# State-space stage of a four-layer gated network: the product with B on VectorE, from PSUM, in place of GpSimd

## The chip, the cores and the metric

The kernel runs on one core of a Trainium2 chip. The metric is the device time of one execution in microseconds (us); the kernel before was timed in three runs. TensorE (PE) multiplies matrices, VectorE (DVE), ScalarE (ACT) and GpSimd (POOL) work element by element, SyncE (SP) issues the transfers. Each engine runs its own instructions in their order and waits for semaphores that others raise.

## The reference

Four layers act on a residual x of 1024 tokens by 256; each adds a gated mixer and a gated feed-forward block. The change lies in the first mixer, a selective state-space model. Cut to that:

```python
x = einsum('ed,bld->bel', in_proj_w, ctx)          # 256 channels
u = silu(causal_conv4(x) + conv_b)
x_dbl = einsum('ke,bel->bkl', x_proj_w, u)         # dt (8), B (16), C (16)
delta = softplus(dt_proj_w @ dt + dt_proj_b)
A = -exp(A_log)                                    # 256 x 16
# for every token, in order, per channel e and state n:
dA = exp(delta * A)
state = state * dA + (delta * u) * B
y = sum over n of state * C
# then
out = (y + D * u) * silu(layernorm(residual))
residual = residual + tanh(g) * out
```

All else (a quantised feed-forward block, attention over 16 heads, experts, two more attention and feed-forward layers) comes after this stage and is the same in both kernels.

## The kernel before

The program runs four stages, `ORDER = ["M", "F0", "A1", "F"]`. The change touches stage M, the state-space mixer, alone. Between stages every engine waits in `begin` for `pe_step`, `act_step`, `dve_step` and, for the stages where GpSimd takes part, `pool_step`.

In M the 256 channels lie on 128 partitions times two (`e`), and the 1024 tokens are cut into two halves of 512. The states are taken one at a time: a step `g` of 32 is half `g // 16` and state `g % 16`, and its tiles are 128 x 1024 float32 (two channel groups of 512 tokens). What a step does, by engine:

- TensorE broadcasts row B of the state to all partitions (`broadcast_B`, L406, a matmul with a selector matrix, into PSUM bank 2 or 3 by turns), and row C in the same way (L428, bank 4 or 5). It runs three broadcasts of B ahead. It then adds the step's result to the sum over the states by multiplying with the identity (L434, two matmuls, each recorded as two; banks 0 and 1).
- ScalarE computes `dA`, the exponential, in two instructions (L836), and copies the broadcast B from PSUM to one of three tiles `Bs` in SBUF (`copy_B`, its record is the helper's L750).
- GpSimd multiplies `du` (delta times u) by the copied B into `dBu` (L1656), two tiles by turns.
- VectorE does the recurrence over the tokens as one scan (L1197) on `dA` and `dBu`, and multiplies the state of the step before by the broadcast C straight from PSUM into `hC` (L1204).

The order on VectorE in iteration g is: the scan of g, then the product with C of g - 1, then what is due beside. The order on TensorE in iteration g is: broadcast B for g + 3, broadcast C for g, wait for `m_hC` of g - 1, its identity matmuls, then what is due beside. A broadcast of B waits for the copy of the B two before it, the copy for the product three before it, the product for the scan two before it.

Work of other stages is put beside the loop. Sixteen matmuls of the attention's value weights (L445) stand behind the identity matmuls of the steps in `VALUE_AT`, which are 0, 2, ... 14 and 22 to 29; ScalarE copies each two steps later. Behind step 5 stands a small matmul that sums weight magnitudes (L450), behind step 18 the eight transposes of `output(0)` (L414). On VectorE `gated(0)` (L1181, L1186) stands behind the product of step 16, `residual` (L1087) behind iteration 20, the statistics of the next norm behind 21, `normalise` (L1074) behind 24. GpSimd's `rstd_of()` for that norm is issued behind its product of step 23. Ahead of the loop VectorE finishes `delta(0)` and `delta(1)`, which make `du` for the two halves (L1166, L1167, L1172). After it come `gated(1)`, which waits for the last identity matmuls, and ScalarE's rounding of the first feed-forward weights.

Of the kernel before, what the change touches and what calls it, by code (L numbers as in the profile page):

```python
# [14 lines left out]
def flamingo_kernel(nc, dram, out):  # L15
# [5 lines left out]
    ALU, ACT = mybir.AluOpType, mybir.ActivationFunctionType  # L21
# [181 lines left out]
    def S(name):  # L203
        if name not in sems:
            sems[name] = stack.enter_context(nc.semaphore(name))
        return sems[name]
# [48 lines left out]
    def bc(ap, shape):  # L255
        return ap.to_broadcast(shape)
# [107 lines left out]
    def _(pe):  # L364
# [16 lines left out]
        def ssm(k):  # L381
            loaded(pe, "ctxT", "m_in")
            for h in range(2):
                for e in range(2):
                    last = mm(ps[:, 4 * h + e, :], m_in[:, e * P:(e + 1) * P], ctxT[:, h * HALF:(h + 1) * HALF], start=True, stop=True)
                last.then_inc(S("m_x"), 1)
            loaded(pe, "m_bc", "m_dt", "m_dtw")
            for h in range(2):
                pe.wait_ge(S("m_u"), h + 1)
                for e in range(2):  # L390
                    mm(ps[0:96, 2 + 4 * h, :], m_bc[:, e, :], u[h][:, e, :], start=e == 0, stop=e == 1)
                for e in range(2):
                    last = mm(ps[0:8, 3 + 4 * h, :], m_dt[:, e, :], u[h][:, e, :], start=e == 0, stop=e == 1)
                last.then_inc(S("m_dbl"), 1)
                pe.wait_ge(S("m_dts"), h + 1)
                for e in range(2):
                    last = mm(ps[:, 4 * h + e, :], m_dtw[:, e * P:(e + 1) * P], dts[:, :], start=True, stop=True)
                last.then_inc(S("m_dpre"), 1)
            pe.wait_ge(S("m_bcs"), 2)
            pe.wait_ge(S("m_xs"), 2)  # L400
            loaded(pe, "sel_bc", "ident")

            def broadcast_B(g):
                if g >= 2:
                    pe.wait_ge(S("m_Bcopy"), g - 1)
                mm(ps[:, 2 + g % 2, :], sel_bc[:, g % NS, :], bcs[g // NS][:, :], start=True, stop=True).then_inc(S("m_B"), 1)  # L406

            def output(h):

                pe.wait_ge(S("m_yz"), h + 1)  # L410
                for t in range(TH):
                    b, lb = t // 2, t % 2
                    for e in range(2):
                        last = nc.tensor.transpose(ps[:, 6 + t // 2, (t % 2) * DM + e * P:(t % 2) * DM + (e + 1) * P],  # L414
                                                   u[h][:, e, b * DM + lb * P:b * DM + (lb + 1) * P], ident[:, :])
                return last

            loaded(pe, "wvT0", "wo0")
            broadcast_B(0)
            broadcast_B(1)  # L420
            broadcast_B(2)
            for g in range(2 * NS + 1):
                if g + 3 < 2 * NS:
                    broadcast_B(g + 3)
                if g < 2 * NS:
                    if g >= 2:
                        pe.wait_ge(S("m_hC"), g - 1)
                    mm(ps[:, 4 + g % 2, :], sel_bc[:, NS + g % NS, :], bcs[g // NS][:, :], start=True, stop=True).then_inc(S("m_C"), 1)  # L428
                if g:
                    pe.wait_ge(S("m_hC"), g)  # L430
                    if g == NS + 1:
                        pe.wait_ge(S("m_y_read"), 1)
                    for e in range(2):
                        last = mm(ps[:, e, :], ident[:, :], hC[(g - 1) % 2][:, e, :], start=(g - 1) % NS == 0, stop=(g - 1) % NS == NS - 1)  # L434
                    last.then_inc(S("m_y"), 1)
                if g in VALUE_AT:
                    v = VALUE_AT.index(g)
                    if v == HEADS // 2:
                        loaded(pe, "wvT1", "wo1")
                        pe.wait_ge(S("m_res"), 1)  # L440
                    if v >= 2:
                        pe.wait_ge(S("wvo_copied"), v - 1)
                    if v == 3:
                        pe.wait_ge(S("w_scales"), 1)
                    mm(ps[:, 6 + v % 2, 0:DM], wvT[:, v % (HEADS // 2), :], wo[:, v % (HEADS // 2), :], start=True, stop=True).then_inc(S("wvo_psum"), 1)  # L445
                if g == 5:
                    pe.wait_ge(S("wvo_copied"), 2)
                    pe.wait_ge(S("wabs_part"), 1)
                    pe.wait_ge(S("ones_set"), 1)
                    mm(ps[:, 7, 256:259], ones[:, :], wabs[:, 0:3], start=True, stop=True).then_inc(S("wabs_sum"), 1)  # L450
                if g == NS + 2:
                    pe.wait_ge(S("wvo_copied"), HEADS // 2)
                    output(0).then_inc(S("m_out"), 1)
            pe.wait_ge(S("wvo_copied"), HEADS)
            output(1).then_inc(S("pe_step"), 1)
# [288 lines left out]
    def _(act):  # L744
# [4 lines left out]
        def copy(out_, in_):  # L749
            return A(out_, in_, ACT.Copy)  # L750
# [16 lines left out]
        def ssm(k):  # L767
# [47 lines left out]
                act.wait_ge(S("m_ln"), h + 1)  # L815
                A(inv, lnw, ACT.Exp, scale=-1.0).then_inc(S("m_lnw"), 1)

            def copy_B(g):
                act.wait_ge(S("m_B"), g + 1)
                if g >= 3:  # L820
                    act.wait_ge(S("m_dBu"), g - 2)
                copy(Bs[g % 3][:, :], ps[:, 2 + g % 2, :]).then_inc(S("m_Bcopy"), 1)

            act.wait_ge(S("m_bcs"), 2)
            copy_B(0)
            copy_B(1)
            link(sum_weights(1))
            sum_weights(2).then_inc(S("wabs_part"), 1)
            for g in range(2 * NS):
# [7 lines left out]
                             dlt[h][:, e, :].rearrange("p (b l) -> p b l", b=2)[:, :, 1:DM],  # L837
                             ACT.Exp, scale=negA[:, e, n:n + 1])
                last.then_inc(S("m_dA"), 1)
                if g + 2 < 2 * NS:  # L840
                    copy_B(g + 2)
                if g - 2 in VALUE_AT:
                    v = VALUE_AT.index(g - 2)
                    act.wait_ge(S("wvo_psum"), v + 1)
# [210 lines left out]
    def _(dve):  # L1055
# [53 lines left out]
        def ssm(k):  # L1109
# [67 lines left out]
            def gated(h):  # L1177
# [9 lines left out]
                                           xn[h][:, :, :].rearrange("p (b e) l -> p e b l", e=2)[:, e], ALU.mult)  # L1187
                last.then_inc(S("m_yz"), 1)

            flat = "p e t -> p (e t)"  # L1190
            for g in range(2 * NS + 1):
                if g < 2 * NS:
                    dve.wait_ge(S("m_dA"), g + 1)
                    dve.wait_ge(S("m_dBu"), g + 1)
# [342 lines left out]
    def _(pool):  # L1537
# [67 lines left out]
        for k, s in enumerate(ORDER):  # L1605
# [42 lines left out]
                continue  # L1648
            if s == "M":
                begin(pool, k)  # L1650
                for g in range(2 * NS):
                    pool.wait_ge(S("m_Bcopy"), g + 1)
                    pool.wait_ge(S("m_du"), g // NS + 1)
                    if g >= 2:
                        pool.wait_ge(S("m_h"), g - 1)
                    G.tensor_tensor(dBu[g % 2][:, :, :], du[g // NS][:, :, :], bc(Bs[g % 3][:, :].unsqueeze(1), [P, 2, HALF]),  # L1656
                                    ALU.mult).then_inc(S("m_dBu"), 1)
                    if g == NS + 7:
                        rstd_of()
                pool.wait_ge(S("m_dBu"), 2 * NS)  # L1660
                G.tensor_copy(scratch[:, 16:17], mhalf[:, 0:1]).then_inc(S("pool_step"), 1)

    stack.close()
# [105 lines left out]
```

## Time and profile before

| | us |
|---|---|
| median of 3 runs | 1192.35 |
| lowest, highest | 1190.04, 1193.18 |
| profiled execution, span from its first to its last instruction | 1197.3 |
| busy over the whole span: TensorE | 1019.5 |
| VectorE | 773.8 |
| ScalarE | 649.2 |
| GpSimd | 521.5 |

The profiled execution's own time is known by its span, the last row of the first block; it lies 5 us above the median of the runs. All durations come from that one execution. The loop of stage M begins at 61 us (the first scan) and ends at 212 us (the last product with C). "PEclk" is the clock that TensorE was granted, as a share of 2.4 GHz: 1.00 is the full level, 0.50 the low one of 1.2 GHz, and a number between is the mean of a stretch with both. In the timeline each line is an instruction, or some of the same kind merged (x2, x4), with its start and its length; square brackets hold the engine's idle time before it and who ended it. A float32 matmul has two records, so one step's identity matmuls are four.

### The profile page before, as it was taken

What the parts mean: (1) busy time and instruction counts of PE and PEld (TensorE: products, weight loads), DVE (VectorE), ACT (ScalarE), POOL (GpSimd) and SP (SyncE); (2) the same over time, 40 slices, a digit from 0 to 9 for tenths busy, and PEclk for the clock granted to TensorE, in tenths of its full rate; (3) what the DMA queues carried; (4) which work ended last, traced back from release to release, by engine and by line L of the source; (5) the groups of instructions that cost most, each with busy time, mean ns of one, the idle gap of its engine ahead of it and who ended that gap; (6) DMA issues with size and microseconds to landing.
All of it is one profiled execution on the core that took longest, in us unless ns stands there. A gap on an engine that the chain in (4) does not pass through costs nothing.

```text
span 1197.3 us, 15768 instructions
## 1 busy us (share of the span) xinstructions
PE 1019.5 (85%) x5576; PEld 811.0 (68%) x5576; DVE 773.8 (65%) x1276; ACT 649.2 (54%) x1261; POOL 521.5 (44%) x513
## 2 busy tenths in 40 slices
PE   5367677465899999899987899988999999999898
PEld 1022233134799999799976787867777788778787
DVE  6799999794455555655535655577565666667565
ACT  3834434574577667667653466743656644433443
POOL 0254454002466666556643234334344445334353
PEclk7567878785799999999997999998999999989999
DMA  9000100003400000000004000000000040000000
GB/s 353 22 0 1 53 1 1 0 1 130 185 1 1 1 2 1 1 1 1 1 1 193 1 1 1 1 1 1 1 1 1 11 187 1 1 1 1 1 18 19
DMA packets 4734, 35.84 MB, mean 30 GB/s; under 512 B 1160, under 2 KB 2192, under 8 KB 3152
## 3 DMA queue, kind: packets, MB, share of 16 engines
q1 hardware_dynamic: 4656, 34.83, 7.4%
q8 instruction: 45, 0.74, 0.3%
q14 instruction: 33, 0.27, 0.1%
HBM read 33.78 MB, written 1.05 MB: 29 GB/s over the span
## 4 chain that ended last, share of the span: by engine, by line
PE 52%; DVE 14%; ACT 5%; issue 5%; DVEq 0%; POOL 0%; ACTq 0%; POOLq 0%
PE psum L377 13%; PE psum L379 12%; PE psum L378 12%; PE psum L605 4%; DVE f_h_lo L1515 3%; PE psum L593 2%; PE psum L548 2%; ACT f_silu L1032 2%; DVE f_silu L1498 2%; DVE x_norm L1074 2%; PE psum L552 1%; DVE f_silu L1507 1%; PE psum L669 1%; PE psum L704 1%; ACT a_P L948 1%
## 5 line engine op out<-in xcount | busy, mean ns | idle before, releaser
L377 PE MATMUL psum<-x_norm_T_hi,f_wgu_hi 128*128 128x512 f32 x400 | 178.2, 445 | 0.0
L1507 DVE TENSOR_TENSOR f_silu<-f_silu,psum 128x512 f32<-128x512 f32 x100 | 68.8, 688 | 167.8 <-ACT f_silu L1032 167.8
L379 PE MATMUL psum<-x_norm_T_hi,f_wgu_lo 128*128 128x512 f32 x400 | 161.7, 404 | 0.0
L378 PE MATMUL psum<-x_norm_T_lo,f_wgu_hi 128*128 128x512 f32 x400 | 161.2, 403 | 0.0
L750 ACT ACTIVATE f_h_hi<-f_silu 128x512 fp32r<-128x512 f32 x100 | 63.0, 630 | 172.6 <-DVE f_silu L1498 172.1
L377 PE MATMUL psum<-f_wd_hi,f_h_hi 128*128 128x256 f32 x400 | 121.6, 304 | 13.2 <-DVE f_h_lo L1515 13.1
L1515 DVE TENSOR_TENSOR f_h_lo<-f_silu,f_h_hi 128x512 fp32r<-128x512 f32 x100 | 123.6, 1236 | 3.6 <-ACT f_h_hi L750 3.5
L434 PE MATMUL psum<-m_hC,ident_f 128*128 128x512 f32 x128 | 83.7, 790 | 48.4 <-DVE m_hC L1204 46.1
L1584 POOL TENSOR_TENSOR f_wgu_lo<-f_wa,f_wgu_hi 128x512 fp32r<-128x512 f32 x44 | 56.6, 1287 | 146.4 <-ACT f_wgu_hi L750 146.3
L1656 POOL TENSOR_TENSOR m_dBu<-m_du,m_Bs 128x1024 f32<-128x1024 f32 x32 | 79.0, 2471 | 90.2 <-DVE m_h L1197 34.9
L378 PE MATMUL psum<-f_wd_lo,f_h_hi 128*128 128x256 f32 x400 | 114.1, 285 | 0.0
L379 PE MATMUL psum<-f_wd_hi,f_h_lo 128*128 128x256 f32 x400 | 113.8, 285 | 0.0
L1584 POOL TENSOR_TENSOR f_wgu_lo<-f_w,f_wgu_hi 128x512 fp32r<-128x512 f32 x44 | 56.6, 1287 | 103.8 <-ACT f_wgu_hi L750 103.7
L377 PEld LDWEIGHTS psum<-f_wd_hi,f_h_hi 128*128 128x128 f32 x400 | 77.3, 193 | 23.6 <-issue 21.0
L1032 ACT ACTIVATE f_silu<-psum 128x512 f32<-128x512 f32 x100 | 59.1, 591 | 62.7 <-PE psum L379 56.7
L1629 POOL TENSOR_TENSOR a_P<-a_P,a_row_inv 128x1024 f32<-128x1024 f32 x32 | 60.7, 1896 | 71.6 <-DVE a_row_inv L1357 71.6
L379 PEld LDWEIGHTS psum<-x_norm_T_hi,f_wgu_lo 128*128 128x128 f32 x400 | 77.7, 194 | 18.4
L378 PEld LDWEIGHTS psum<-x_norm_T_lo,f_wgu_hi 128*128 128x128 f32 x400 | 78.5, 196 | 15.8
L377 PEld LDWEIGHTS psum<-x_norm_T_hi,f_wgu_hi 128*128 128x128 f32 x400 | 79.2, 198 | 14.6 <-POOL f_wgu_lo L1584 0.2
L434 PEld LDWEIGHTS psum<-m_hC,ident_f 128*128 128x128 f32 x128 | 26.7, 229 | 88.3 <-DVE m_hC L1204 63.8
L378 PEld LDWEIGHTS psum<-f_wd_lo,f_h_hi 128*128 128x128 f32 x400 | 77.5, 194 | 3.9 <-issue 1.4
L379 PEld LDWEIGHTS psum<-f_wd_hi,f_h_lo 128*128 128x128 f32 x400 | 77.4, 193 | 0.0
(297 smaller groups left out, 2794.1 us busy)
## 6 DMA issues: line engine op xcount, KB each, us to landing
f_wa<-in_f1a SPq DMA_DIRECT2D x1, 8448.0 KB, 24.8
f_w<-in_f3w SPq DMA_DIRECT2D x1, 5376.0 KB, 17.0
w_raw<-in_w0raw SPq DMA_DIRECT2D x1, 3072.0 KB, 16.2
f_w<-in_f2w SPq DMA_DIRECT2D x1, 3072.0 KB, 14.5
f_wb<-in_f1b SPq DMA_DIRECT2D x1, 2304.0 KB, 8.2
a_wo<-in_wo SPq DMA_DIRECT2D x2, 1024.0 KB, 12.0
a_wq<-in_wq SPq DMA_DIRECT2D x1, 2048.0 KB, 24.6
x_res<-in_x SPq DMA_DIRECT2D x1, 1024.0 KB, 7.8
```

Of the source, the lines that this page charges most:

```text
L377: mm(out, wh, xh, start=start, stop=False, **kw)
L378: mm(out, wh, xl, start=False, stop=False, **kw)
L379: return mm(out, wl, xh, start=False, stop=stop, **kw)
L434: last = mm(ps[:, e, :], ident[:, :], hC[(g - 1) % 2][:, e, :], start=(g - 1) % NS == 0, stop=(g - 1) % NS == NS - 1)
L605: last = mm(ps[:, 4, b * DM:(b + 1) * DM], ctk[:, ((i - 1) // HEADS) * TH + 2 * b + kv, :], PT[:, b, kv * DM:(kv + 1) * DM], start=kv == 0 ...
L750: return A(out_, in_, ACT.Copy)
L1032: A(sg[g % 2][:, :], ps[:, 2 + 2 * (g % 2), :], ACT.Silu).then_inc(S("f_sg"), 1)
L1507: V.tensor_tensor(sg[g % 2][:, :], sg[g % 2][:, :], ps[:, 3 + 2 * (g % 2), :], ALU.mult).then_inc(S("f_m"), 1)
L1515: V.tensor_tensor(hl[(g - 1) % 2][:, :], sg[(g - 1) % 2][:, :], hh[(g - 1) % 2][:, :].bitcast(f32), ALU.subtract).then_inc(S("f_hl"), 1)
L1584: G.tensor_tensor(wgl[g % 2][:, :], raw_w(l, j)[:, 0:GU], wgh[g % 2][:, :].bitcast(f32), ALU.subtract).then_inc(S("f_wg"), 1)
L1629: G.tensor_tensor(Pm[i % 2][:, :, :], Pm[i % 2][:, :, :], bc(ri[:, :].unsqueeze(2), [P, TH, DM]), ALU.mult).then_inc(S("a_pn"), 1)
L1656: G.tensor_tensor(dBu[g % 2][:, :, :], du[g // NS][:, :, :], bc(Bs[g % 3][:, :].unsqueeze(1), [P, 2, HALF]), ALU.mult).then_inc(S("m_dBu"), 1)
```

## The change

VectorE gets a new function, `input_term(g)`, that multiplies `du` by the broadcast B read from PSUM and writes `dBu`. It is issued one step ahead: for step 0 before the loop, and for g + 1 at the head of iteration g, ahead of the scan of g. GpSimd's product and ScalarE's copy of B are gone, and with them the wait of the broadcast for the copy: it now waits for the product two steps before it. TensorE's broadcast of B runs one step ahead of its iteration in place of three: two before the loop, then B for g + 1 at the head of iteration g. GpSimd's `rstd_of()` comes first in its stage.

```diff
--- before.py
+++ after.py
@@ -402,7 +402,7 @@
 
             def broadcast_B(g):
                 if g >= 2:
-                    pe.wait_ge(S("m_Bcopy"), g - 1)
+                    pe.wait_ge(S("m_dBu"), g - 1)
                 mm(ps[:, 2 + g % 2, :], sel_bc[:, g % NS, :], bcs[g // NS][:, :], start=True, stop=True).then_inc(S("m_B"), 1)
 
             def output(h):
@@ -418,10 +418,9 @@
             loaded(pe, "wvT0", "wo0")
             broadcast_B(0)
             broadcast_B(1)
-            broadcast_B(2)
             for g in range(2 * NS + 1):
-                if g + 3 < 2 * NS:
-                    broadcast_B(g + 3)
+                if g and g + 1 < 2 * NS:
+                    broadcast_B(g + 1)
                 if g < 2 * NS:
                     if g >= 2:
                         pe.wait_ge(S("m_hC"), g - 1)
@@ -815,15 +814,6 @@
                 act.wait_ge(S("m_ln"), h + 1)
                 A(inv, lnw, ACT.Exp, scale=-1.0).then_inc(S("m_lnw"), 1)
 
-            def copy_B(g):
-                act.wait_ge(S("m_B"), g + 1)
-                if g >= 3:
-                    act.wait_ge(S("m_dBu"), g - 2)
-                copy(Bs[g % 3][:, :], ps[:, 2 + g % 2, :]).then_inc(S("m_Bcopy"), 1)
-
-            act.wait_ge(S("m_bcs"), 2)
-            copy_B(0)
-            copy_B(1)
             link(sum_weights(1))
             sum_weights(2).then_inc(S("wabs_part"), 1)
             for g in range(2 * NS):
@@ -837,8 +827,6 @@
                              dlt[h][:, e, :].rearrange("p (b l) -> p b l", b=2)[:, :, 1:DM],
                              ACT.Exp, scale=negA[:, e, n:n + 1])
                 last.then_inc(S("m_dA"), 1)
-                if g + 2 < 2 * NS:
-                    copy_B(g + 2)
                 if g - 2 in VALUE_AT:
                     v = VALUE_AT.index(g - 2)
                     act.wait_ge(S("wvo_psum"), v + 1)
@@ -1187,8 +1175,19 @@
                                            xn[h][:, :, :].rearrange("p (b e) l -> p e b l", e=2)[:, e], ALU.mult)
                 last.then_inc(S("m_yz"), 1)
 
+            def input_term(g):
+                dve.wait_ge(S("m_du"), g // NS + 1)
+                dve.wait_ge(S("m_B"), g + 1)
+                if g >= 2:
+                    dve.wait_ge(S("m_h"), g - 1)
+                V.tensor_tensor(dBu[g % 2][:, :, :], du[g // NS][:, :, :], bc(ps[:, 2 + g % 2, :].unsqueeze(1), [P, 2, HALF]),
+                                ALU.mult).then_inc(S("m_dBu"), 1)
+
             flat = "p e t -> p (e t)"
+            input_term(0)
             for g in range(2 * NS + 1):
+                if g + 1 < 2 * NS:
+                    input_term(g + 1)
                 if g < 2 * NS:
                     dve.wait_ge(S("m_dA"), g + 1)
                     dve.wait_ge(S("m_dBu"), g + 1)
@@ -1648,16 +1647,7 @@
                 continue
             if s == "M":
                 begin(pool, k)
-                for g in range(2 * NS):
-                    pool.wait_ge(S("m_Bcopy"), g + 1)
-                    pool.wait_ge(S("m_du"), g // NS + 1)
-                    if g >= 2:
-                        pool.wait_ge(S("m_h"), g - 1)
-                    G.tensor_tensor(dBu[g % 2][:, :, :], du[g // NS][:, :, :], bc(Bs[g % 3][:, :].unsqueeze(1), [P, 2, HALF]),
-                                    ALU.mult).then_inc(S("m_dBu"), 1)
-                    if g == NS + 7:
-                        rstd_of()
-                pool.wait_ge(S("m_dBu"), 2 * NS)
+                rstd_of()
                 G.tensor_copy(scratch[:, 16:17], mhalf[:, 0:1]).then_inc(S("pool_step"), 1)
 
     stack.close()
```

## Rows read from the trace of the kernel before

**Rows 1.** The page's first line.
```profile
span 1197.3 us, 15768 instructions
```

**Rows 2.** Stretches: us, busy (x count) by engine, PEclk, DMA share, GB/s.
```profile
50.00:65.00 15.00, 3.41 (x7) 1.04 (x7) 14.84 (x10) 10.40 (x16) 8.03 (x3) 0.50 0.00 1
65.00:212.00 147.00, 105.46 (x219) 41.40 (x220) 142.50 (x84) 62.64 (x105) 75.95 (x32) 0.79 0.03 11
```

**Rows 3.** Timeline of one step: start us, us, engine, line, what, [idle before].
```profile
100.04 1.19 DVE L1204 TENSOR_TENSOR m_hC<-m_inv,psum 128x1024 f32<-128x1024 f32 x1
...
100.28 2.36 POOL L1656 TENSOR_TENSOR m_dBu<-m_du,m_Bs 128x1024 f32<-128x1024 f32 x1 [2.31 <-DVE m_h L1197]
...
101.28 3.20 PE L434 MATMUL psum<-m_hC,ident_f 128*128 128x512 f32 x4 [2.26 <-DVE m_hC L1204]
101.36 3.43 DVE L1197 TENSOR_TENSOR_SCAN m_inv<-m_dA,m_dBu 128x1024 f32<-128x1024 f32 x1
...
104.71 1.19 DVE L1204 TENSOR_TENSOR m_hC<-m_h,psum 128x1024 f32<-128x1024 f32 x1
```

**Rows 4.** Groups by line, 50 to 215 us: busy us, mean ns, idle before.
```profile
L1656 POOL TENSOR_TENSOR m_dBu<-m_du,m_Bs 128x1024 f32<-128x1024 f32 x32 | 79.0, 2471 | 90.2 <-DVE m_h L1197 34.9 <-DVE m_inv L1197 31.3 <-DVE m_du L1172 21.7
...
L750 ACT ACTIVATE m_Bs<-psum 128x512 f32<-128x512 f32 x32 | 18.9, 594 | 72.1 <-PE psum L406 72.1
```

**Rows 5.** Timeline of VectorE, scans and products with no GpSimd product beside them.
```profile
61.01 2.28 DVE L1197 TENSOR_TENSOR_SCAN m_h<-m_dA,m_dBu 128x1024 f32<-128x1024 f32 x1
63.21 2.26 DVE L1197 TENSOR_TENSOR_SCAN m_inv<-m_dA,m_dBu 128x1024 f32<-128x1024 f32 x1
...
210.13 1.20 DVE L1204 TENSOR_TENSOR m_hC<-m_h,psum 128x1024 f32<-128x1024 f32 x1
...
211.24 1.22 DVE L1204 TENSOR_TENSOR m_hC<-m_inv,psum 128x1024 f32<-128x1024 f32 x1
```

**Rows 6.** Timeline of VectorE ahead of the loop, alone and beside GpSimd.
```profile
50.87 1.22 DVE L1167 TENSOR_TENSOR m_delta<-m_delta,m_du 128x1024 f32<-128x1024 f32 x1
...
54.53 3.27 DVE L1167 TENSOR_TENSOR m_delta<-m_delta,m_du 128x1024 f32<-128x1024 f32 x1
...
57.83 3.25 DVE L1172 TENSOR_TENSOR m_du<-m_delta,m_u 128x1024 f32<-128x1024 f32 x1
```

**Rows 7.** Timeline, product to copy of B, low clock.
```profile
65.39 1.19 DVE L1204 TENSOR_TENSOR m_hC<-m_h,psum 128x1024 f32<-128x1024 f32 x1
...
66.63 3.78 PE L434 MATMUL psum<-m_hC,ident_f 128*128 128x512 f32 x4 [8.50 <-DVE m_hC L1204]
...
70.88 0.60 ACT L750 ACTIVATE m_Bs<-psum 128x512 f32<-128x512 f32 x1 [4.05 <-PE psum L406]
```

**Rows 8.** The same, full clock, its product in rows 3.
```profile
105.95 1.98 PE L434 MATMUL psum<-m_hC,ident_f 128*128 128x512 f32 x4
...
108.19 0.60 ACT L750 ACTIVATE m_Bs<-psum 128x512 f32<-128x512 f32 x1 [0.46 <-PE psum L406]
```

**Rows 9.** The same with a value matmul between, low and then full clock.
```profile
184.47 3.78 PE L434 MATMUL psum<-m_hC,ident_f 128*128 128x512 f32 x4 [3.00 <-DVE m_hC L1204]
...
189.57 0.60 ACT L750 ACTIVATE m_Bs<-psum 128x512 f32<-128x512 f32 x1 [4.90 <-PE psum L406]
...
193.81 1.98 PE L434 MATMUL psum<-m_hC,ident_f 128*128 128x512 f32 x4 [0.86 <-DVE m_hC L1204]
...
196.48 0.60 ACT L750 ACTIVATE m_Bs<-psum 128x512 f32<-128x512 f32 x1 [1.62 <-PE psum L406]
```

**Rows 10.** Timeline, work beside the loop, and the last two sums.
```profile
143.22 1.39 DVE L1181 SCALAR_TENSOR_TENSOR m_delta<-m_u,small_params,psum 128x512 f32<-128x512 f32 x2
...
152.54 1.32 PE L414 MATMUL psum<-ident_f,m_u 128*128 128x128 f32 x8
...
178.49 2.62 DVE L1074 TENSOR_SCALAR x_norm<-x_res,bn_mv,rstd 128x256 f32<-128x256 f32 x4
...
211.38 3.70 PE L434 MATMUL psum<-m_hC,ident_f 128*128 128x512 f32 x8 [1.33 <-DVE m_hC L1204]
```

## The prediction

> **What bounds the kernel now.** I read the page first. The stage that the diff touches is a small part of the whole [rows 1]; everything behind it is untouched, so only the stage's length counts, and what it hands on. Then the busy time by stretches: between 65 and 212 us VectorE is busy 142.50 of 147.00 us and TensorE 105.46, at a granted clock of 0.79, a mix of its two levels, 1.2 and 2.4 GHz; just before, with TensorE busy 3.41 of 15 us, it was 0.50 [rows 2]. VectorE bounds this stage.
>
> The timeline shows one step of the 32. VectorE does one product with C (1.19 us) and one scan (3.43 us); the next product starts 4.67 us after the last. GpSimd's product (2.36 us) starts as soon as the scan before has ended and lies beside the next scan. TensorE starts its sum over the state, the identity matmuls of L434, 0.05 us after the product with C has ended [rows 3]. By groups, GpSimd's 32 products take 79.0 us, ScalarE's 32 copies of B 18.9 us [rows 4]. Neither ends a wait of VectorE: its rows show no idle time ahead of scan or product [rows 3].
>
> But GpSimd's product does cost VectorE. Scans with no GpSimd product beside them take 2.28 and 2.26 us and the next starts 2.20 us later [rows 5], against 3.43 us with one [rows 3]. The same holds for products: 1.22 us alone, 3.27 and 3.25 us beside the first two GpSimd products [rows 6].
>
> **The change, part by part.** I write D(g) for the product with B, S(g) for the scan, H(g) for the product with C, Y(g) for the identity matmuls.
>
> *VectorE's own work.* Before, a step is 4.67 us. After it is D + S + H. D has the shape and operand places of H (one operand in SBUF, one in PSUM, 1024 elements): 1.19 us, and the next instruction can start 1.11 us after it starts [rows 5]. With S at 2.20 from start to start a step is 1.11 + 2.20 + 1.11 = 4.42 us: 0.25 us less. The 32 x 1.11 = 36 us added are paid by 32 scans freed of some 1.15 us each, or 37 us. The trace says that a PSUM operand costs nothing here: 1.19 us [rows 3] against 1.22 us for the same product with both operands in SBUF [rows 6]. The Trainium skill, "VectorE: DVE Perf Modes", section "The TRN2 errata", gives 120 fixed cycles from PSUM and 58 from SBUF; by that page the moved product would be 0.065 us dearer than one from SBUF, an estimate of 2 us over 32. The trace disagrees, so I add nothing.
>
> *The start.* delta(1) no longer runs beside GpSimd: two products of 3.27 and 3.25 us become 1.22 each [rows 6], 4.1 us less; D(0) and D(1) now come between it and S(0), 2.2 us, and D(2) has to wait for S(0) and stands ahead of S(1) and H(0). Counted from 54.53: L1172 at 55.8, D(0) 57.0, D(1) 58.1, S(0) 59.2, D(2) 61.5, S(1) 62.6, H(0) 64.8. H(0) ends at 66.0, where it now ends at 66.58 [rows 7]: -0.5 us.
>
> *The new wait; here lies the result.* Before, TensorE ran three broadcasts of B ahead, and two copies in SBUF stood ready. After, broadcast B(g+1) is issued at the head of TensorE's iteration g. TensorE is in order: ahead of B(g+1) stands Y(g-2) of iteration g-1, and that waits for H(g-2). On VectorE, H(g-2) is the last instruction ahead of D(g+1). So D(g+1) can't start when H(g-2) ends: it waits until TensorE has done Y(g-2), where there is one the value-weight matmul (L445), and B(g+1). While VectorE computes, TensorE has only the C broadcast to do; while TensorE computes, VectorE waits. Queued behind D(g+1) are S(g) and H(g-1), and behind H(g-1) again Y(g-1): the two engines take turns. The other order would have been B ahead of Y.
>
> The price stands in the trace of before, since there too B's broadcast follows Y; the start of ScalarE's copy says when B was there. At the low clock: H ends at 66.58, the copy starts at 70.88, 4.30 us [rows 7]. At the full clock: H ends at 104.71 + 1.19 = 105.90 [rows 3], the copy starts at 108.19, 2.29 us [rows 8]. With a value matmul between: 0.05 + 5.10 = 5.15 us low, 0.05 + 2.67 = 2.72 us full [rows 9], so 0.85 or 0.43 us more. D(3) to D(31) wait so: 29 times. Of the 16 value matmuls 15 stand ahead of such a B (the first stands ahead of B(2)). Once the wait holds Y(16) until gated(0) has read the sums, 1.4 us, and once output(0)'s eight transposes, 1.3 us, stand ahead of B(20) [rows 10]. Sum of the waits, all low: 29 x 4.30 + 15 x 0.85 + 2.7 = 140.2 us. All full: 29 x 2.29 + 15 x 0.43 + 2.7 = 75.6 us.
>
> *The sum.* From the end of one H to the end of the next is the wait + 1.11 + 2.20 + 1.19 = wait + 4.50 us. H(29) ends at 66.0 + 29 x 4.50 + waits = 196.5 + waits, H(30) 3.3 us later and H(31) 1.1 us after that (no D is left): 200.9 + waits. Now H(31) ends at 211.24 + 1.22 = 212.46 [rows 5]. Change: waits - 11.6 us. The last two Y took 3.70 us at the full clock [rows 10]; at the low one they take some 3 us more, since a slow Y takes twice as long. So +64.0 us all full, +131.6 us all low.
>
> *Which clock.* Today, with TensorE busy 72% of the stretch, the clock was 0.79, so 58% of it full; with 23% it was 0.50 [rows 2]. In the new step TensorE works some 4.7 us (4.25 us from Y's start to the copy's at the low clock [rows 7], and the C broadcast) out of 4.30 + 4.50 = 8.8, or 53%. On the straight line between the two rows 53% gives 0.68, so 36% full. I take 25%, my choice: where the full clock comes only after a burst of work, part of it is spent in the pause: 0.75 x 131.6 + 0.25 x 64.0 = 114.7 us.
>
> *Side work of VectorE* (quantise_weights, the second half of gated(0), residual, statistics, normalise) lies in the new waits and costs nothing. Without that cover it is some 9 us, an estimate: the first half of gated(0) takes 1.39 us and normalise 2.62 [rows 10]; the second half of gated(0), the residual and the statistics are passes of like length over the same tiles.
>
> *ScalarE* loses 18.9 us of copies [rows 4]; its exponentials start at the end of a scan and are done long before the next but one. Nobody waits for them, so 0. Its rounding of the weights after the loop (12 us) starts during the last waits, still done before VectorE's gated(1): 0. *GpSimd* loses 79.0 us and issues its rstd ahead of time, where it waits for statistics that now come later; nothing else is queued behind it in this stage: 0. Its pool_step is early: 0. *SP* and the DMAs: no instruction is moved past them; the second half of the value weights waits for value copies that come late by half the loss and is needed only in the second half: 0.
>
> Against the profiled execution, whose span is 1197.3 us, 114.7 us give a span of 1312; its time is not listed beside its span, so I add the difference to the median of 1192.35, which lies 5 us below the span: 1307 us.
>
> **The rivals.**
> A, the forecast: turns taken, with the clock at both levels. 62%, +100 to +125 us.
> B: every burst at the low clock, +131.6 us, 1324 us. For it: between 66 and 71 us Y ran throughout at the low clock after a long pause [rows 7], and the new pause is over 4 us in every step. Against it: today's pauses of some 2 us [rows 3] did not keep the clock from rising. By the Trainium skill, "TensorE: Matmul & The Clock Gate", section "HAM oscillation", bursts parted by waits each start cold again; by it this rival would hold in every step. 20%.
> C: mostly the full clock, +64 to +98 us, 1256 to 1290 us. For it: the full clock gave a Y of 1.98 us [rows 8] in a loop where TensorE idles for over a quarter of the time [rows 2]. Against it: in the new step it idles for half. 14%.
> D, the other side: B is in PSUM before H(g-2) ends, and VectorE runs gap-free. It decides at one place, whether B(g+1) gets ahead of Y(g-2) on TensorE. Then 30 steps gain 0.25 us and the start 0.5, 8 us in all, of which up to 5 go to side work (steps that hold some had their scan free of GpSimd already, and gain nothing): -3 to -8 us, 1184 to 1189 us. Against it: the program's order and the wait of Y for H, and broadcasts and Y that stand in program order in the trace [rows 7, 8]. 4%.
>
> **How the numbers follow.** The likeliest is A: 1307 us. A measurement can tell some 0.3%, 3.6 us, from no change. The range takes the upper half of C, A, and B with 5 us for effects on the clock behind the stage: 1270 to 1329. D is split evenly: faster 0.02, same 0.02, slower 0.96.
>
> **What would show it.** Right: steps of 7 to 10 us instead of 4.67; VectorE idle before the new product (D), released by TensorE's L406, 3 to 5 us each time and some 100 to 140 us in all; scans at 2.28 us throughout; D at 1.19 us; VectorE busy in the stage about as before; the granted clock of the stage at 0.5 to 0.75; all stages behind it as long as now. Wrong: D following H within 0.1 us (rival D), scans still at 3.4 us without GpSimd, D much dearer than H although its form is the same, or a loss behind the stage.

## The result, and the profile after

The changed kernel takes 1320.95 us (median of four runs, 1319.21 to 1321.61), the kernel before 1191.36 us in the runs beside it: a ratio of 1.1081, with a 95% interval of 1.1066 to 1.1097. The change costs 129.6 us. Forecast were 1307 us and a range of 1270 to 1329.

The page of the changed kernel, its span and the busy time of the engines:

```profile
span 1319.8 us, 15706 instructions
...
PE 1053.3 (80%) x5576; PEld 821.4 (62%) x5576; DVE 775.1 (59%) x1308; ACT 634.3 (48%) x1229; POOL 438.6 (33%) x481
```

VectorE is as busy as before (775.1 us against 773.8), GpSimd is 83 us lighter, and the span is 122.5 us longer than that of [rows 1]. So it is a loss by waiting. The stretch of the loop, as in [rows 2] (busy us by engine, then PEclk, DMA share, GB/s):

```profile
65.00:338.00 273.00, 144.51 (x222) 54.82 (x223) 144.14 (x112) 53.85 (x78) 1.14 (x2) 0.66 0.02 6
```

VectorE, which was busy 142.50 of 147 us, is busy for 144.14 of 273; TensorE 144.51; the granted clock has gone from 0.79 to 0.66. The waits in the stage (who waited for whom: us in total, times, the longest):

```profile
PE psum L433 <- DVE m_hC L1203: 128.8, 29, 7.0
DVE m_dBu L1183 <- PE psum L406: 120.7, 27, 5.2
```

The second line did not exist before. The first is its other half: TensorE waits for VectorE for about as long. One turn, to be read beside [rows 3] and [rows 7] (start us, us, engine, line, what, [idle before]):

```profile
64.79 1.20 DVE L1203 TENSOR_TENSOR m_hC<-m_h,psum 128x1024 f32<-128x1024 f32 x1
...
66.04 3.78 PE L433 MATMUL psum<-m_hC,ident_f 128*128 128x512 f32 x4 [6.96 <-DVE m_hC L1203]
...
69.62 0.63 PE L406 MATMUL psum<-m_bc_split,sel_bc 96*128 96x512 bf16 x1
...
70.34 1.22 DVE L1183 TENSOR_TENSOR m_dBu<-m_du,psum 128x1024 f32<-128x1024 f32 x1 [4.36 <-PE psum L406]
...
73.69 1.20 DVE L1203 TENSOR_TENSOR m_hC<-m_inv,psum 128x1024 f32<-128x1024 f32 x1
```

The product with C ends at 65.99. TensorE's identity matmuls start 0.05 us later, the broadcast of B comes behind them, and VectorE's product with B, which stands next on VectorE, starts at 70.34: a wait of 4.35 us, for which the forecast had 4.30 from [rows 7]. Then product, scan and product follow without a gap. With a value matmul between:

```profile
91.28 1.20 DVE L1203 TENSOR_TENSOR m_hC<-m_inv,psum 128x1024 f32<-128x1024 f32 x1
...
97.69 1.22 DVE L1183 TENSOR_TENSOR m_dBu<-m_du,psum 128x1024 f32<-128x1024 f32 x1 [5.21 <-PE psum L406]
```

97.69 - 92.48 = 5.21 us; forecast 5.15 from [rows 9]. The new products and the scans, by tile (duration ns min/median/max, first and last start):

```profile
L1183 DVE TENSOR_TENSOR m_dBu<-m_du,psum x32: 1215/1222/1222, 56.8 to 328.2; 128x1024 f32<-128x1024 f32 x32
L1196 DVE TENSOR_TENSOR_SCAN m_h<-m_dA,m_dBu x16: 2283/2284/2286, 59.0 to 329.4; 128x1024 f32<-128x1024 f32 x16
```

No scan is above 2.29 us, where [rows 3] had 3.43; a product with B takes 1.22 us.

The stage in three parts, against the kernel before. To the first scan: 59.03 us against 61.01 [rows 5]. From there to the end of the last product with C: 338.34 - 59.03 = 279.3 us against 151.5. From there to the end of the span: 981.5 us against 984.8. The loop alone is 127.8 us longer. Other kernels of this study have 978.9 to 984.7 us in the third part with the same program there, so a difference of 3 us there is no effect that can be told.

### The profile page after: what moved, and what is told of

Read it like the earlier page. It is cut to its first block, busy times and chain, and to the rows that moved or that the text cites. A ratio compares the mean times of both kernels' runs of the same rounds, so it can differ in the third digit from the quotient of the medians.

```text
span 1319.8 us, 15706 instructions
## 1 busy us (share of the span) xinstructions
PE 1053.3 (80%) x5576; PEld 821.4 (62%) x5576; DVE 775.1 (59%) x1308; ACT 634.3 (48%) x1229; POOL 438.6 (33%) x481
## 4 chain that ended last, share of the span: by engine, by line
PE 47%; DVE 12%; ACT 5%; issue 5%; DVEq 0%; POOL 0%; ACTq 0%; POOLq 0%
PE psum L377 12%; PE psum L378 11%; PE psum L379 11%; PE psum L604 4%; DVE f_h_lo L1514 3%; PE psum L592 2%; PE psum L547 2%; ACT f_silu L1020 2%; DVE f_silu L1497 2%; DVE x_norm L1062 1%; PE psum L551 1%; DVE f_silu L1506 1%; PE psum L668 1%; PE psum L703 1%; ACT a_P L936 1%
## 5 line engine op out<-in xcount | busy, mean ns | idle before, releaser
L433 PE MATMUL psum<-m_hC,ident_f 128*128 128x512 f32 x128 | 114.7, 1050 | 134.4 <-DVE m_hC L1203 128.8
L433 PEld LDWEIGHTS psum<-m_hC,ident_f 128*128 128x128 f32 x128 | 36.8, 316 | 190.1 <-DVE m_hC L1203 151.6
L1544 POOL TENSOR_TENSOR rstd<-var_eps,minus_half 128x4 f32<-128x4 f32 x16 | 16.1, 1008 | 397.7 <-DVE var_eps L1057 397.6
L826 ACT ACTIVATE m_dA<-m_delta,neg_A 128x510 f32<-128x510 f32 x64 | 42.5, 712 | 161.8 <-DVE m_h L1196 98.4
L1183 DVE TENSOR_TENSOR m_dBu<-m_du,psum 128x1024 f32<-128x1024 f32 x32 | 39.0, 1221 | 127.9 <-PE psum L406 120.7
L1020 ACT ACTIVATE f_silu<-psum 128x512 f32<-128x512 f32 x100 | 59.2, 592 | 62.6 <-PE psum L379 56.5
```

The costliest lines, as they stand in the source:

```text
L826: last = A(dA[g % 2][:, e, :].rearrange("p (b l) -> p b l", b=2)[:, :, 1:DM], dlt[h][:, e, :].rearrange("p (b l) -> p b l", b=2)[:, :, 1:D ...
L1020: A(sg[g % 2][:, :], ps[:, 2 + 2 * (g % 2), :], ACT.Silu).then_inc(S("f_sg"), 1)
```

## The experiments

The theory: the loss is one of order. B stands behind Y on TensorE, Y waits for the product with C, and that stands next to the product with B on VectorE. Rival 1: VectorE got 36 us of products more, and the time is theirs. Rival 2: TensorE's clock fell, and that is the loss by itself. All ratios are to the kernel before, run beside each kernel on the same chip.

**The broadcast one step further ahead** (two_ahead). One edit on TensorE:

```diff
-                if g and g + 1 < 2 * NS:
-                    broadcast_B(g + 1)
+                if g + 2 < 2 * NS:
+                    broadcast_B(g + 2)
```

> The changed kernel with one thing moved: TensorE issues the broadcast of B for g + 2 (not g + 1) at the head of iteration g, so it stands ahead of the identity matmuls of the step before and not behind them. Order theory (the loss is VectorE's wait for a B that stands behind Y): the waits before the product with B, 120.7 us in all, fall to a few us, a step takes 4.42 us at the full clock and up to 5.2 us where TensorE runs low with a value matmul; total 1180 to 1200 us. Rival 1 (the 32 products cost VectorE what they last, 36 us or more, whatever the order): not under 1225 us. Rival 2 (TensorE's low clock is the loss, by itself): the clock in the loop stays near 0.55 and the time above 1250 us.

Measured: 1186.98 us, ratio 0.9967 (0.9955 to 0.9980); run again in a later group 1187.87 us, 0.9963 (0.9944 to 0.9982). VectorE's rows of one step, then the whole loop as a stretch (us, busy by engine, PEclk):

```profile
120.01 1.20 DVE L1203 TENSOR_TENSOR m_hC<-m_inv,psum 128x1024 f32<-128x1024 f32 x1
...
121.12 1.22 DVE L1183 TENSOR_TENSOR m_dBu<-m_du,psum 128x1024 f32<-128x1024 f32 x1
...
122.25 2.29 DVE L1196 TENSOR_TENSOR_SCAN m_inv<-m_dA,m_dBu 128x1024 f32<-128x1024 f32 x1
...
124.45 1.20 DVE L1203 TENSOR_TENSOR m_hC<-m_h,psum 128x1024 f32<-128x1024 f32 x1
```
```profile
56.00:206.00 150.00, 103.41 (x225) 41.02 (x224) 148.03 (x116) 51.25 (x80) 1.15 (x2) 0.80 0.03 11
```

Steps are 4.44 us, and the loop lasts 150.2 us. VectorE is busy 148.03 of 150 us. The broadcast for the state after next still stands behind Y of two steps back, but has a whole step to arrive. The loss of 130 us is gone with this edit alone, with all 32 products still on VectorE: rival 1 falls, and the order stands. Of rival 2 only its forecast falls here (a clock near 0.55 and over 1250 us), for the clock came back to 0.80 with the same edit; what the clock costs by itself is told by fill_more below. Rival D could not come about in the changed kernel's own order; with the order that it supposed, the time is the one that the forecast had put on it, 1184 to 1189 us.

**Each product twice** (product_twice), to price VectorE's part by itself: two_ahead with a second product over the first.

```diff
+                link(V.tensor_tensor(dBu[g % 2][:, :, :], du[g // NS][:, :, :], bc(ps[:, 2 + g % 2, :].unsqueeze(1), [P, 2, HALF]), ALU.mult))
                 V.tensor_tensor(dBu[g % 2][:, :, :], du[g // NS][:, :, :], bc(ps[:, 2 + g % 2, :].unsqueeze(1), [P, 2, HALF]),
```

> two_ahead with each product with B computed twice on VectorE, the second over the first and after it. Theory (with B there in time VectorE bounds the loop, and a product costs what it lasts): the 32 more cost 1.11 to 1.3 us each, +36 to +42 us, 1223 to 1229 us. That is what rival 1 could have cost at most. If VectorE does not bound the loop: under +15 us.

Measured: 1229.76 us, ratio 1.0318 (1.0292 to 1.0344), 41.9 us above two_ahead in the runs beside it (1187.87) and 0.8 above the range expected. By the traces 2.5 us are the two products ahead of the loop and 3 lie behind it. VectorE's rows:

```profile
100.17 1.19 DVE L1204 TENSOR_TENSOR m_hC<-m_h,psum 128x1024 f32<-128x1024 f32 x1
...
101.28 1.21 DVE L1183 TENSOR_TENSOR m_dBu<-m_du,psum 128x1024 f32<-128x1024 f32 x1
...
102.53 1.22 DVE L1184 TENSOR_TENSOR m_dBu<-m_du,psum 128x1024 f32<-128x1024 f32 x1
...
105.86 1.19 DVE L1204 TENSOR_TENSOR m_hC<-m_inv,psum 128x1024 f32<-128x1024 f32 x1
```

The step is 105.86 - 100.17 = 5.69 us, 1.25 us more: 1.11 of the product and 0.14 of the wait between the two. The loop grew by 36.2 us (186.4 against 150.2). So the products do cost their 36 us. In the change they are paid for by what GpSimd's product no longer holds back: in the trace of before, 25 of the 32 scans took longer than 2.3 us, 30 us more in sum than at 2.28 us each, and the two products of [rows 6] took 4.1 us more.

**The value matmuls out of the chain** (value_early): the block that issues them is moved from behind the identity matmuls to ahead of the wait for `m_hC`.

```diff
+                if g in VALUE_AT:
+                    ...
                 if g:
                     pe.wait_ge(S("m_hC"), g)
                     ...
-                if g in VALUE_AT:
-                    ...
```

> The changed kernel with the sixteen value-weight matmuls issued ahead of TensorE's wait for the product with C, in its idle time, not behind the identity matmuls. Order theory: 15 waits lose 0.85 us each (low clock), 13 us in all, 1308 us; the waits of 5.2 us become 4.35. Rival 1: no change, 1321 us.

Measured: 1311.14 us, ratio 1.1008 (1.0992 to 1.1025): 9.8 us less than the change, where 13 were expected. The loop is 8.9 us shorter. One of the missing microseconds is seen in step 6 (TensorE's value and identity matmuls):

```profile
106.67 1.19 PE L437 MATMUL psum<-a_wo,a_wvT 128*128 128x256 f32 x2 [4.84 <-DVE w_inv L1088]
...
107.65 3.54 PE L443 MATMUL psum<-m_hC,ident_f 128*128 128x512 f32 x4
```

The fourth value matmul waits for the weight scale, which VectorE computes behind the product with C. The product with C had ended at 106.25, so the identity matmuls start 1.4 us after it and not 0.05. The rest was not taken apart. A likely part of it, not shown: some value matmuls of the changed kernel ran at the full level, where one adds 0.43 us to the wait and not 0.85.

**TensorE kept at work in its pause** (fill_c, and fill_more with 14 in place of 7 or 8). The repeats write what the last one writes, so nothing in the result changes.

```diff
+                    for _ in range(7 if g in VALUE_AT else 8):
+                        mm(ps[:, 4 + g % 2, :], sel_bc[:, NS + g % NS, :], bcs[g // NS][:, :], start=True, stop=True)
                     mm(ps[:, 4 + g % 2, :], sel_bc[:, NS + g % NS, :], bcs[g // NS][:, :], start=True, stop=True).then_inc(S("m_C"), 1)
```

> The changed kernel with the broadcast of C repeated 7 or 8 times more into the same bank in each step, in TensorE's idle time while VectorE computes; the same result, only to keep TensorE at work. Theory (the wait is as long as Y and B at the granted clock): if the clock stays at the full level the waits go from 4.35 us (5.2 with a value matmul) to 2.3 (2.7), 1255 to 1275 us; in between if it is full only in part. Rival 1: no change, 1321 us. If the fillers do not raise the clock at all: 1321 us, since they fit in the pause even at the low clock.

Measured: 1294.05 us, ratio 1.0871 (1.0854 to 1.0889). The stretch of the loop, and the identity matmuls of one step:

```profile
65.00:310.00 245.00, 167.18 (x439) 66.92 (x440) 142.26 (x110) 52.97 (x77) 1.14 (x2) 0.83 0.02 7
```
```profile
120.06 3.48 PE L435 MATMUL psum<-m_hC,ident_f 128*128 128x512 f32 x4 [2.44 <-DVE m_hC L1205]
```

The mean clock rose to 0.83, above the 0.79 of [rows 2], and yet Y took 3.48 us here, and in other steps from 1.98 to 3.78 us: the mean does not say at which level Y runs. VectorE's waits for B still sum to 94.1 us. The time lies between the two that were expected for a full clock and for none.

> The kernel fill_c with 14 repeated broadcasts of C a step in place of 7 or 8, so that TensorE is at work up to the end of the product with C once its clock is full. Theory (the wait is Y and B at the granted clock, and 64 us is its price at the full one): with the clock full almost throughout the waits are 2.3 us (2.7 with a value matmul), 70 to 80 us in all, 1250 to 1270 us. If the low clock goes on in part, the 14 last 6 us there and are longer than the pause, so those steps are over 1 us longer and the time may be above fill_c's 1294 us.

Measured: 1261.33 us, ratio 1.0582 (1.0557 to 1.0608). The stretch of the loop (its PEclk is the third number from the end), and the ends of products with C with the starts of the products with B behind them:

```profile
56.00:281.00 225.00, 179.95 (x657) 77.24 (x655) 150.00 (x116) 56.56 (x82) 1.15 (x2) 0.98 0.02 7
```
```profile
136.15 1.20 DVE L1205 TENSOR_TENSOR m_hC<-m_h,psum 128x1024 f32<-128x1024 f32 x1
...
139.70 1.22 DVE L1185 TENSOR_TENSOR m_dBu<-m_du,psum 128x1024 f32<-128x1024 f32 x1 [2.35 <-PE psum L406]
...
143.04 1.19 DVE L1205 TENSOR_TENSOR m_hC<-m_inv,psum 128x1024 f32<-128x1024 f32 x1
...
147.01 1.22 DVE L1185 TENSOR_TENSOR m_dBu<-m_du,psum 128x1024 f32<-128x1024 f32 x1 [2.78 <-PE psum L406]
```

The time is within the range expected. With the clock at 0.98 the wait is 2.35 us (139.70 - 137.35) and, with a value matmul, 2.78 us (147.01 - 144.23); forecast from [rows 8, 9] 2.29 and 2.72. The waits that end on B sum to 70.2 us, the loop is 225.3 us. So of the 127.8 us that the change adds to the loop, some 54 belong to the low clock and 74 stay with the clock almost always full. That settles rival 2: the wait itself, not the clock, is the larger part.

**The old products with the new order** (before_one_ahead): the kernel before, with the broadcast one step ahead.

```diff
-            broadcast_B(2)
             for g in range(2 * NS + 1):
-                if g + 3 < 2 * NS:
-                    broadcast_B(g + 3)
+                if g and g + 1 < 2 * NS:
+                    broadcast_B(g + 1)
```

On ScalarE the copy of a value matmul changes places with `copy_B(g + 2)`.

> The kernel before, products still on GpSimd and copies on ScalarE, with TensorE's broadcast of B one step ahead as in the change (and ScalarE's copy of a value matmul moved ahead of its copy of B, as that order needs). Order theory: from the end of one product with C to the scan two steps on there are now Y and B (4.3 us low, 2.3 full), the copy 0.6 and GpSimd's product 2.4, then a scan and a product: 4.9 us (full) to 6.0 us (low) a step in place of 4.67, 1200 to 1230 us. Rival 1: as before, 1191 us, since no product was moved.

Measured: 1361.80 us, ratio 1.1434 (1.1411 to 1.1458): 170 us, 130 more than the upper end expected. Both theories missed the size. The waits, and one step:

```profile
DVE m_h L1196 <- ACT m_dA L835: 88.0, 15, 7.0
DVE m_inv L1196 <- ACT m_dA L835: 87.6, 14, 7.8
```
```profile
105.39 1.19 DVE L1203 TENSOR_TENSOR m_hC<-m_h,psum 128x1024 f32<-128x1024 f32 x1
...
106.63 3.64 PE L433 MATMUL psum<-m_hC,ident_f 128*128 128x512 f32 x4 [6.15 <-DVE m_hC L1203]
...
110.25 0.38 PE L406 MATMUL psum<-m_bc_split,sel_bc 96*128 96x512 bf16 x1
...
111.15 1.32 ACT L835 ACTIVATE m_dA<-m_delta,neg_A 128x510 f32<-128x510 f32 x2
111.33 2.34 POOL L1655 TENSOR_TENSOR m_dBu<-m_du,m_Bs 128x1024 f32<-128x1024 f32 x1 [8.02 <-ACT m_Bs L749]
...
112.50 3.32 DVE L1196 TENSOR_TENSOR_SCAN m_h<-m_dA,m_dBu 128x1024 f32<-128x1024 f32 x1 [5.93 <-ACT m_dA L835]
```

The scan waits for ScalarE's exponential, not for GpSimd's product: 88.0 + 87.6 us. ScalarE is in order too, and its copy for g + 2 stands ahead of the exponential of g + 1. So a step is product, Y (3.64), B, copy, exponential (1.32), scan (3.32): from 105.39 to 115.75, 10.4 us. I had reckoned over two steps with what feeds the product, and overlooked what is queued behind the waiting copy. The order costs the kernel with GpSimd's product 170 us and the changed one, which has taken the copy out, 130.

**GpSimd's product beside two products from PSUM** (pool_idle_product): two_ahead, with GpSimd making a product of the old size that nobody reads, paced by the scans as before.

```diff
+                for g in range(2 * NS):
+                    pool.wait_ge(S("m_du"), g // NS + 1)
+                    if g >= 2:
+                        pool.wait_ge(S("m_h"), g - 1)
+                    G.tensor_tensor(idle_t[:, :, :], du[g // NS][:, :, :], bc(ctxT[:, 0:HALF].unsqueeze(1), [P, 2, HALF]), ALU.mult).then_inc(S("m_idle"), 1)
+                    pool.wait_ge(S("m_idle"), g + 1)
...
```

> The kernel two_ahead with one thing added: in each step GpSimd makes a product of the old size (two inputs in SBUF) that nobody reads, started at the same event as before, the end of a scan. Theory A (GpSimd's product holds back only a scan or a product that reads both inputs from SBUF, and only while it runs): between one scan and the next there are now 2.2 us of products that read PSUM, so of 2.36 us only some 0.2 us fall on the scan: scans 2.3 to 2.6 us, +5 to +12 us, 1192 to 1199 us. Theory B (each GpSimd product costs the scan 1.15 us wherever it lies): scans 3.4 us, +35 us, 1222 us.

Measured: 1200.85 us, ratio 1.0080 (1.0051 to 1.0109). One step, then a product ahead of the loop:

```profile
99.84 1.19 DVE L1205 TENSOR_TENSOR m_hC<-m_inv,psum 128x1024 f32<-128x1024 f32 x1
...
100.08 2.37 POOL L1656 TENSOR_TENSOR m_idle<-m_du,ctx_T 128x1024 f32<-128x1024 f32 x1 [2.32 <-DVE m_h L1198]
100.95 1.21 DVE L1185 TENSOR_TENSOR m_dBu<-m_du,psum 128x1024 f32<-128x1024 f32 x1
...
102.08 2.52 DVE L1198 TENSOR_TENSOR_SCAN m_inv<-m_dA,m_dBu 128x1024 f32<-128x1024 f32 x1
```
```profile
51.28 3.26 DVE L1157 TENSOR_TENSOR m_delta<-m_delta,m_du 128x1024 f32<-128x1024 f32 x1
```

GpSimd's product ends at 102.45; the two VectorE products beside it, each with one operand in PSUM, keep their 1.19 and 1.21 us, and the scan takes 2.52 us in place of 2.28. The loop grew by 6.1 us, not 35: theory A. Ahead of the loop, where both operands lie in SBUF, the same GpSimd product makes 3.26 us of 1.22, and the loop starts 4 us later. Theory A had left those 4 us out, and the time is 1.9 us above its range. The Trainium skill, "SBUF — State Buffer", section "SBUF: two separate sides", describes an exclusive lock on a shared port pair, taken by a GpSimd instruction or by a VectorE one with two SBUF inputs, the loser blocked until the other ends. These rows agree with it: the scan ends 2.15 us after GpSimd's product (104.60 - 102.45), as it does in [rows 3] (104.79 - 102.64), though it starts 2.0 us into that product here and 1.1 us into it there, and takes 2.52 us in place of 3.43.

**Half the products on GpSimd** (split, and split_first_on_dve). The even states' products go to GpSimd and their B is copied by ScalarE again, with broadcasts four ahead and a third tile for the product; the odd ones stay on VectorE. The core of it:

```diff
+                ahead = g + 2 if g % 2 else g + 4
+                if ahead < 2 * NS:
+                    broadcast_B(ahead)
...
-                if g + 1 < 2 * NS:
+                if g % 2 == 0 and g + 1 < 2 * NS:
                     input_term(g + 1)
...
+                for g in range(0, 2 * NS, 2):
+                    ...
+                    if g >= 3:
+                        pool.wait_ge(S("m_h"), g - 2)
+                    G.tensor_tensor(dBu[g % 3][:, :, :], du[g // NS][:, :, :], bc(Bs[g // 2 % 2][:, :].unsqueeze(1), [P, 2, HALF]),
...
```

> A version meant to beat both: the product with B of the odd states on VectorE from PSUM (as in the change, B two steps ahead), that of the even states on GpSimd from ScalarE's copy (B four ahead), with a third tile for the product, in the space of the padded input, so that GpSimd can start its product at the end of the scan three steps before, beside two VectorE products that read PSUM. Theory A of pool_idle_product: two steps are 2 x (2.20 + 1.11) + 1.11 + 0.2 = 7.9 us in place of 8.9, up to 15 us less than two_ahead, 1172 us, less where TensorE at the low clock (4.3 us a step, 5.1 with a value matmul) becomes the bound: 1172 to 1187 us. Theory B: 1.15 us a pair comes back, 1187 us or more.

Measured: 1186.37 us, ratio 0.9943 (0.9921 to 0.9964). Two steps:

```profile
109.77 1.19 DVE L1217 TENSOR_TENSOR m_hC<-m_inv,psum 128x1024 f32<-128x1024 f32 x1
...
113.55 2.36 POOL L1669 TENSOR_TENSOR m_dBu<-m_du,m_Bs 128x1024 f32<-128x1024 f32 x1 [5.99 <-DVE m_inv L1210]
...
114.41 1.22 DVE L1198 TENSOR_TENSOR m_dBu<-m_du,psum 128x1024 f32<-128x1024 f32 x1
...
115.54 2.52 DVE L1210 TENSOR_TENSOR_SCAN m_h<-m_dA,m_xpad 128x1024 f32<-128x1024 f32 x1
...
117.99 1.19 DVE L1217 TENSOR_TENSOR m_hC<-m_inv,psum 128x1024 f32<-128x1024 f32 x1
```

117.99 - 109.77 = 8.2 us for two steps, where two_ahead has 8.9 and 7.9 were expected, and the loop lasts 141.9 us, 8 less. But it starts 3 us later, since GpSimd's first product again falls on the products of delta(1), and the third part of the span is 983.8 us, against 978.9 in two_ahead. The whole is no faster than two_ahead beyond what can be told.

> The kernel split with the product with B of state 0 on VectorE too, and GpSimd's first product held back until both halves' inputs are ready, so that it no longer falls on the products of delta(1), which took over 3 us there. Theory (GpSimd's product holds back VectorE only where both inputs are in SBUF): the loop starts 3 us earlier and lasts as long as in split, 142 us: 1181 to 1185 us, under two_ahead by 2 to 6 us. Rival: the gain in the loop is given back behind it, no difference to two_ahead.

Here the first product is VectorE's and GpSimd waits for `m_du` to reach 2. Measured: 1186.50 us, ratio 0.9949 (0.9928 to 0.9971), two_ahead beside it 0.9963 (0.9944 to 0.9982). That is 1.5 us above the range expected. The loop does start 3.3 us earlier (55.69), but lasts 147.8 us, 5.9 more than in split. Some 2.2 us of that are GpSimd's first product, which now falls on the second scan (4.44 us against 2.26), and some 4 are longer idle times of VectorE, whose cause was not looked into. The intervals overlap almost wholly, so a gain over two_ahead isn't shown.

**Both edits on TensorE** (two_ahead_value_early).

> two_ahead with the value matmuls ahead of TensorE's wait for the product with C. In two_ahead two waits of 0.7 us are left, one of them in a value step; total 1185 to 1187 us, no change beyond what can be told.

Measured: 1188.04 us, ratio 0.9960 (0.9944 to 0.9977): 1 us above the range expected, and no change against two_ahead that can be told.

## Why the prediction was right, and where it was off

*The wait and its place* were right: B(g+1) behind Y(g-2) behind H(g-2), next to D(g+1) on VectorE. The rows of the changed kernel show it, and two_ahead, which changes only that order, takes it all away. 29 waits were forecast; the trace has 29 (27 put down to the broadcast, and two, behind gated(0) and normalise, to issue).

*The prices* were right to 0.06 us: 4.35 and 5.21 us at the low clock, and, measured in fill_more, 2.35 and 2.78 at the full one.

*VectorE's own work*: the product costs 1.11 to 1.14 us from start to start, the scan 2.20, the step 4.44 us in two_ahead against 4.42 forecast. One reading was loose: 25 scans were held by GpSimd's product, not 32, and they gave back 30 us, not 37. The Trainium skill, "VectorE: DVE Perf Modes", section "The TRN2 errata", would have made the product from PSUM dearer than one from SBUF. The trace disagrees: the product from PSUM took 1.22 us against the 1.22 us of [rows 6], so the row was the better guide.

*The start* came out as forecast:

```profile
54.37 1.23 DVE L1155 TENSOR_TENSOR m_delta<-m_delta,m_du 128x1024 f32<-128x1024 f32 x1
...
56.77 2.35 DVE L1183 TENSOR_TENSOR m_dBu<-m_du,psum 128x1024 f32<-128x1024 f32 x2
...
59.03 2.29 DVE L1196 TENSOR_TENSOR_SCAN m_h<-m_dA,m_dBu 128x1024 f32<-128x1024 f32 x1
```

The scan starts at 59.03 (forecast 59.2), the first product with C ends at 65.99 (forecast 66.0). That it fits so closely is partly luck: in two_ahead, value_early and fill_more, with the same work ahead of the loop, the first scan starts at 56.0 us, and in fill_c at 57.9.

*The clock* is the term that was mis-sized: the share of the waits at the full level, of which the forecast says "I take 25%, my choice". From the end of a product with C to the start of the product with B behind it, the 29 waits sum to 135.2 us, side work included. The formula gives 140.2 us all low and 75.6 all full, and 124 with a quarter full; 135.2 is 8% full. The mean clock had been forecast well (0.68 by the line, 0.66 measured). What went wrong is where in the step the full level falls. Two bursts of TensorE, each with the pause behind it (PEclk third from the end):

```profile
119.50:124.90 5.40, 4.13 (x6) 1.46 (x6) 1.21 (x2) 1.33 (x2) 0.00 (x0) 0.50 0.02 3
124.90:128.40 3.50, 0.50 (x2) 0.00 (x0) 3.33 (x2) 0.00 (x0) 0.00 (x0) 0.91 0.00 0
138.10:143.20 5.10, 3.80 (x6) 1.42 (x6) 1.25 (x2) 1.33 (x2) 0.00 (x0) 0.56 0.00 0
143.20:146.60 3.40, 0.21 (x1) 0.00 (x0) 3.32 (x2) 0.00 (x0) 0.00 (x0) 0.92 0.00 0
```

The bursts ran at 0.50 and 0.56, the pauses behind them at 0.91 and 0.92. Over the 29 waits the full level was granted for 7% of the time, and between them for 58%; in 5 of the 28 stretches between them it was not granted at all. In most turns of this loop the clock had risen by the time the burst was over, and was low again for the next. That is all but rival B, with 1324 us; it had a chance of 20% and should have had the larger one. The Trainium skill, "TensorE: Matmul & The Clock Gate", section "HAM oscillation", tells of bursts parted by waits that each start cold. The trace agrees in the main: 17 of the 29 waits had no full clock at all, and in none was the mean clock above 0.69.

*The sum*, put right: waits of 135.2 - 11.6 = 123.6 us at the end of the last product with C; measured 338.34 - 212.46 = 125.9. Of the 2.3 us between, 0.9 are the last product's wait for its broadcast of C (second row below), and the rest is 0.04 us more in each turn and 0.2 us ahead of the last scan. The 3 us more for the last two Y did not come:

```profile
336.82 3.78 PE L433 MATMUL psum<-m_hC,ident_f 128*128 128x512 f32 x8
337.12 1.22 DVE L1203 TENSOR_TENSOR m_hC<-m_inv,psum 128x1024 f32<-128x1024 f32 x1 [0.82 <-PE psum L427]
...
340.65 1.41 DVE L1169 SCALAR_TENSOR_TENSOR m_delta<-m_u,small_params,psum 128x512 f32<-128x512 f32 x2 [2.30 <-PE psum L433]
```

(The last two Y, a product with C, and the first half of gated(1).) VectorE goes on 2.3 us after its last product, 2.7 before. The last two Y took 3.78 us, against the 3.70 us of [rows 10], since they ran at the full clock here too: it was 0.95 from 336.80 to 340.60 us.

By spans the loss is 122.5 us, where the forecast had 114.7: the clock gave 11 us more and the turns 2 more, the last two Y some 2 less and the stretch behind the loop 3 less. So part of the clock's error was made up by luck. By medians the loss is 129.6 us. A time is 1.8 us above the span of its execution (1321.61 against 1319.8), so the profiled execution of before took some 1199.1 us, an estimate, 7.7 above the median of 1191.36, while that of the changed kernel lay 0.7 above its own. Adding a difference of spans to the median left these 7 us out.

*Side work* was hidden as forecast: the waits that hold gated(0), the residual, the statistics or normalise are no longer for it than the others, save the one that gated(0) lengthens, 5.73 us, where 4.30 + 1.4 was forecast. (In two_ahead, where no wait covers it, the steps with this work take 5.7 to 7.1 us in place of 4.44.) *ScalarE, GpSimd, SP*: nobody waited for them in the changed kernel.

## What to carry to other kernels

When a producer's lead is cut, write out the in-order queue of the producing engine and ask what stands ahead of the instruction, and what that waits for: here the work on the consumer's own last result stood ahead of the input that it needed next, and one step more of lead gave back all of 130 us. Price such a wait from the old trace, where the same chain often exists as slack, and at the clock of the burst itself, not at the mean of the loop. And ask what is queued behind a waiting instruction on the third engine: in before_one_ahead the copy that waited cost more through the exponential behind it than through its own result.

## What the runs showed that I had not expected

- A mean clock of 0.83 (fill_c) went with identity matmuls of anything from 1.98 to 3.78 us. With 14 repeats in the pause (fill_more, 0.98) they took the full-clock time in nearly every step, although TensorE still idled about 1.4 us ahead of each burst.
- GpSimd's product beside VectorE products that read PSUM costs 6.1 us over 32 steps, and 3.26 us in place of 1.22 for a single product beside it whose operands both lie in SBUF.
- normalise took 1.38 us for four instructions with GpSimd idle, against 2.62 us in [rows 10] with it at work, although each reads one tensor from SBUF, beside two values per partition.
- The stretch behind the loop, the same program in every kernel, varied from 978.9 to 984.8 us. What sets it was not looked into; it is as large as the differences between the versions that beat the kernel before.
